# Row maxima subtracted through four array strips, and a new order around it, in a two-layer decoder kernel

## The reference, cut to what matters

```python
def _layernorm(x, axis=-1, eps=1e-05): ...
# 16 heads of 16 channels, 32 sequences of 128 tokens
scores = jnp.einsum('bhqd,bhkd->bhqk', q, k) / math.sqrt(Hd)
probs = jax.nn.softmax(scores, axis=-1)
out = jnp.einsum('bhqk,bhkd->bhqd', probs, v)
...
x = x + _L0_attn_ref(_layernorm(x), ...)                 # self-attention with rotary factors, 16 heads
x = x + _L0_xattn_ref(_layernorm(x), ctx_1024, ...)      # one wide head, tanh of mixed queries and keys
x = x + _L0_ffn_ref(_layernorm(x), ...)                  # routed feed-forward
x = x + _L1_attn_ref(_layernorm(x), ...)                 # self-attention, 16 heads
x = x + _L1_xattn_ref(_layernorm(x), ctx, ctx, mask, ...)# cross-attention, 16 heads, mask over keys
x = x + _L1_ffn_ref(_layernorm(x), ...)                  # ternary feed-forward
```

## Time and profile before

| | us |
|---|---|
| median of 3 runs | 1351.38 (1351.25 to 1352.72) |
| profiled execution | 1354.58 |
| its span (what the rows below count from) | 1352.7 |
| TensorE busy in the span | 1278.7 (95%) |
| VectorE, ScalarE, GpSimd busy | 986.2, 832.0, 468.1 |

### The profile page before, as it was taken

One profiled execution on the slowest core, in us unless ns is written; L12 is line 12 of the kernel. 1 busy time (PEld: TensorE's weight loads), 2 busy tenths in 40 slices (PEclk: granted clock), 3 DMA queues, 4 the chain that ended last, 5 costly groups with the idle time before them and its releaser, 6 DMA issues. The chain is left out here.

```text
span 1352.7 us, 40285 instructions
## 1 busy us (share of the span) xinstructions
PE 1278.7 (95%) x14932; PEld 1153.3 (85%) x14932; DVE 986.2 (73%) x2421; ACT 832.0 (62%) x1659; POOL 468.1 (35%) x576
## 2 busy tenths in 40 slices
PE   6999999899989999998999999999999998699997
PEld 5888888699979999998898888888777877589987
DVE  7888888456655555564888888887877788568886
ACT  4877777455655454553777777666666676356563
POOL 2232232122222122111000000056655567378884
PEclk9999999999988999999999999999999999899999
DMA  6000000031110000001010000000000000000000
GB/s 239 2 3 0 0 1 2 10 116 39 32 32 1 1 0 0 1 1 56 2 65 0 0 0 3 10 18 17 18 16 16 16 9 3 16 9 31 23 30 35
DMA packets 16884, 29.55 MB, mean 22 GB/s; under 512 B 3744, under 2 KB 7840, under 8 KB 16384
## 3 DMA queue, kind: packets, MB, share of 16 engines
q1 hardware_dynamic: 16768, 27.98, 6.3%
HBM read 23.78 MB, written 4.19 MB: 21 GB/s over the span
## 5 line engine op out<-in xcount | busy, mean ns | idle before, releaser
L853 ACT ACTIVATE a_probs<-a_S 128x512 f32<-128x512 f32 x384 | 205.7, 602 | 86.3 <-PE a_S L1314 46.2
L177 POOL TENSOR_TENSOR all_var_eps<-all_moments,all_ln_eps 128x2 f32<-128x2 f32 x96 | 24.3, 253 | 568.3 <-DVE all_moments L172 556.5
L1055 DVE TENSOR_REDUCE a_row_max<-a_S 128x4 bf16<-128x512 f32 x256 | 164.1, 682 | 16.7 <-PE a_S L1252 16.6
L806 POOL TENSOR_TENSOR a_shifts<-a_add_mask,a_cross_max 128x512 bf16<-128x512 bf16 x128 | 141.7, 1133 | 56.8 <-DVE a_cross_max L1055 56.8
L1326 PE MATMUL a_AV<-a_probs,a_v_pad 128*32 128x128 f32 x3072 | 103.8, 276 | 10.1 <-DVE all_odd_split L1068 6.2
L858 ACT ACTIVATE a_av_raw<-a_AV 128x512 f32<-128x512 f32 x96 | 57.5, 599 | 73.0 <-PE a_AV L1326 73.0
L1261 PE MATMUL a_S<-a_qm_hi,all_odd_split 32*128 32x256 f32 x1536 | 94.2, 301 | 6.0 <-DVE a_row_max L1055 2.2
L1326 PEld LDWEIGHTS a_AV<-a_probs,a_v_pad 128*32 128x32 f32 x3072 | 78.1, 109 | 24.8 <-issue 9.8
L105 PE MATMUL c_OUT<-all_odd_split,c_h_hi 128*128 128x256 f32 x512 | 94.6, 283 | 0.9 <-DVE all_x_res L1995 0.9
L1261 PEld LDWEIGHTS a_S<-a_qm_hi,all_odd_split 32*128 32x128 f32 x1536 | 68.9, 183 | 27.1 <-issue 11.6
L1055 DVE TENSOR_REDUCE a_cross_max<-a_S 128x4 f32<-128x512 f32 x128 | 82.6, 682 | 12.1 <-PE a_S L1284 12.1
(11 more groups left out here) (303 smaller groups left out, 4001.5 us busy)
## 6 DMA issues: line engine op xcount, KB each, us to landing
all_cx<-in_ctx_turned SPq DMA_DIRECT2D x16, 256.0 KB, 2.7
all_cx<-in_ctx SPq DMA_DIRECT2D x16, 256.0 KB, 2.7
out_x<-all_x_res SPq DMA_DIRECT2D x16, 256.0 KB, 2.0
all_x_res<-in_x SPq DMA_DIRECT2D x7, 512.0 KB, 7.4
b_routed_wi<-in_L_ffn_wi_W SPq DMA_DIRECT2D x1, 1024.0 KB, 5.2
b_routed_wo<-in_L_ffn_wo_W SPq DMA_DIRECT2D x1, 1024.0 KB, 8.0
all_even_weights<-in_L_ffn_W_fc SPq DMA_DIRECT2D x1, 1024.0 KB, 4.9
all_even_weights<-in_L_ffn_W_proj SPq DMA_DIRECT2D x1, 1024.0 KB, 6.9
```

Source lines behind the costliest of these rows:

```text
L806: pool.tensor_tensor(shifts[:, j], add_mask[:], cross_max[:, j, :].rearrange("p (h o) -> p h o", o=1).to_broadcast([P, QH, P]), ALU.subtra ...
L853: act.activation(probs[:, b * NQ + j, :], S2[j][:], ACT.Exp, scale=DH ** -0.5).then_inc(exp_ok, 1)
L1055: dve.tensor_reduce((cross_max if at(G)[0].cross else row_max)[:, j, :], S1[j][:].rearrange("p (h k) -> p h k", h=QH), AXX, ALU.max).then_ ...
```

## The change

1. **Self-attention layers, both of them.** The maxima of a sequence are kept in a bf16 tile of 128x(4x32), of which 4 columns in each 32 are filled and the rest is zero (set once by GpSimd). A new `turn_maxima` transposes it by one product with the identity into the fourth S1 bank, as soon as the fourth maximum is there. A new `take_rows` on ScalarE copies these 128x128 values to `max_rows`. `shift_scores` then runs 16 products of 32 rows and 128 columns: strip j holds the rows of bank j, the weights are a column of minus one-hot rows broadcast over 128 columns, and the order is by head first and strip second, so that four neighbouring products lie in four strips. The transposes of the coming group move ahead of the shift in these layers too.
2. **Cross-attention.** On VectorE `normalise_x(G + 3)` moves ahead of `normalise`, and `moments_of(G + 4)` right behind it, ahead of the context's low part.
3. **Starts of the stages.** The first sequence's maxima move ahead (`maxima(0, 0, ...)` in group -1); the first moments are taken before the constants are prepared; the fold runs by halves of the weights, each with its own loads and semaphore; the masks of the cross layer are prepared a group later; the first low parts of stage a1 stand in another order.
4. **Filling products.** `fill` issues products of a tile of ones whose result nobody reads: 22 and 11 in the start of a0, 5 and 3 in the start of a1, 4 at the end of both attention stages.
5. The value bias of the cross layer moves behind the shift of the group where it falls.

The diff, cut to its core:

```diff
+def fill(pe, consts, bank, n):
+    for _ in range(n):
+        pe.matmul(bank[:, 0:P], consts["ones"][:], consts["ones"][:], start=True, stop=True, skip_group_check=True)
...
     def fold(self, dve, turn_sign):
-        dve.wait_ge(self.w_ahead, 16 * len(self.ahead))
...
         for k in range(KC):
+            dve.wait_ge(self.w_ahead[k], 16 * len(self.ahead[k]))
...
-    row_max = sb("row_max", [P, 4, QH], BF16)
+    row_max = sb("row_max", [P, 4, 32], BF16)
+    max_rows = sb("max_rows", [P, P], BF16)
...
+            def take_rows(G, b):
+                act.wait_ge(rows_full, G * PAIR + b + 1)
+                at_least(act, s2_full, step(G, b, 0))
+                act.activation(max_rows[:], S1[NQ - 1][:, 0:P], ACT.Copy).then_inc(rows_ok, 1)
...
+                if inside(G) and not at(G)[0].cross:
+                    take_rows(G, 0)
                 for j in range(NQ):
                     if inside(G):
                         exp_step(G, 0, j)
...
+                early = inside(G + 2) and at(G + 2)[0].cross
+                if early and inside(G + 3):
+                    normalise_x(G + 3)
                 if inside(G):
                     normalise(G * PAIR)
+                if early and inside(G + 4):
+                    moments_of(G + 4)
...
+            def turn_maxima(G, b):
+                pe.wait_ge(max_ok, step(G, b, NQ))
+                pe.matmul(S1[NQ - 1][:, 0:P], row_max[:].rearrange("p j h -> p (j h)"), ident_b[:], start=True, stop=True,
+                          skip_group_check=True).then_inc(rows_full, 1)
...
             def shift_scores(G, b):
-                made, n = at(G)[0].cross, at(G)[1]
+                if not at(G)[0].cross:
+                    pe.wait_ge(rows_ok, G * PAIR + b + 1)
+                    for h in range(QH):
+                        for j in range(NQ):
+                            strip = slice(32 * j, 32 * j + 32)
+                            last = pe.matmul(S2[j][:, h * P:(h + 1) * P], minus_rows_b[strip, h:h + 1].to_broadcast([32, P]),
+                                             max_rows[strip, :], start=False, stop=h == QH - 1, skip_group_check=True)
+                            if h == QH - 1:
+                                last.then_inc(s2_full, 1)
+                    return
...
                 if inside(G):
                     scores(G, 0, parity)
+                    if not at(G)[0].cross:
+                        turn_maxima(G, 0)
...
-                if late and normed_here(G + 2):
+                if normed_here(G + 2):
                     transposes(G + 2)
                 if inside(G):
                     shift_scores(G, 0)
-                if not late and normed_here(G + 2):
-                    transposes(G + 2)
```

More of the change, by code:

```diff
@@ L788, in _ @@
         def _(pool):
+            pool.memset(row_max[:], 0.0).then_inc(rows_zero, 1)
             for i in range(2):
@@ L1162, in first_half @@
                 piece(G, 0)
-                if inside(G + 1):
+                if x_dram is None and at_first(G, -1):
+                    low_k(0, odd)
+                    first.norm.dve_low(dve, 1, FA, first.xT_hi[parity], first.xT_lo[parity])
+                    moments_of(2)
+                    for v in range(HV):
+                        low_q(0, odd, v)
+                elif inside(G + 1):
                     if rope:
```

108 lines of the change are left out of this document (64 added, 44 removed).

## The result

| | before, us | changed, us |
|---|---|---|
| median | 1351.53 (6 runs) | 1358.13 (6 runs, 1355.99 to 1359.46) |
| ratio | | 1.0044, 95% interval 1.0032 to 1.0055 |
| profiled execution | 1354.58 | 1355.99 |
| TensorE busy | 1278.7 | 1265.0 |

The change makes the kernel 0.44% **slower**; the forecast was 1346.9, faster, with a range to 1358. The two profiles differ by 1.4 us only, the medians by 6.6: before's profiled execution took longer than all six of its timed runs, and the changed kernel's was its fastest. So the profiles are read here for what single halves do, and the sum is taken from medians.

The account below looks back on a forecast made before the run. TensorE's list was taken to set the self-attention halves, with the exponentials close beside it. Strips +12, norm order -13.5, starts -3 summed to -4.5 us: 1350.1 profiled, 1346.9 median, own range 1341 to 1353, wider range 1335 to 1358.

Parts of the forecast that it names:

- the cross layer's norm order: Cross layer: VectorE's norm and moments move to where it waits for ScalarE; -13.5 us (-6 to -16).
- the starts: Starts of a0 and a1: filling products raise the clock earlier, maxima move ahead; -3 us together (-6 to -1).
- What bounds the kernel: Self-attention halves: the length of TensorE's list sets them, with the exponentials beside it having little room (0.20 us, first half).
- The shift in strips: Self-attention layers: first halves 0.5 us longer, second 0.1 shorter, +0.4 us a group; +12 us in all (+6 to +21).
- The condition for calling the forecast wrong: Wrong if first-half S1 starts before 4.6 us behind S2, or if the cross group stays over 17.6 us.
- get their maxima in time: Self-attention second halves: no change or 0.1 us less, as those overrunning by a VectorE wait get maxima in time.
- 0.9 a group, times 15: Cross layer: 0.55 us plus 0.35 us gained a group, times 15, giving the norm order's -13.5 us.
- GpSimd keeps the cross layer: Rival, 10%: shifts slow beside VectorE, the fourth is late again; only 0.4 goes, -6 us, total 1354.
- S2 first at about 25 in a0: Sign expected in the changed profile: first second scores of a0 at about 25 us; maxima waited for at 26.64 before.
- the value bias costs 0: Value bias behind the shift: the same products, so 0 us, counted within the starts' term.
- Array-bound: Rival, 6%: S1 does not follow the exponentials, TensorE's shorter list pays -12 in place of +12 us; 1323.
- Late exponentials: Rival, 22%, slower: strip rounds take 0.12 us, leaving them is dearer; +21 in place of +12 us; 1356.

Follow-up runs that it names:

- the masks late: Changed kernel with transposes behind the shift in the self layers and the fourth maximum right behind the third in four places: 1343.90 us, ratio 0.9935.
- the masks back: Changed kernel with transposes behind the shift, the fourth maximum ahead, and the cross layer's masks prepared in group -2 again: 1341.58 us, ratio 0.9922.

## Why the prediction was wrong

The forecast lies 11.2 us under the result (1346.9 against 1358.1). Of that, 6.3 come from the cross layer's norm order, 3 to 4 from the starts, nothing from the strips' sum, and 1 to 2 are in no part that was measured alone.

**What bounds the kernel: right.** Starts, not busy time, told it, and the waits for `a_probs` grew as foreseen.

**The shift in strips: the sum right, its parts not.** Forecast +12, measured +11.7 for the strips alone. Of it the regular groups make up less than half: +0.17 to 0.2 a group and not +0.4. The first exponential came at 2.47 and not 2.60, because the strips are cheaper than taken: they start 1.96 behind S2 (forecast 2.00), and their rounds start 0.06 apart, the last one 2.14 behind S2 and not 2.27. The way back to full height costs less too (0.15 from the last strip's start to the next product, 0.2 in the forecast), but that is not on the exponentials' way. From there the third exponential ended 2.05 later (forecast 2.13). The condition for calling the forecast wrong, S1 before 4.6 behind S2, was met by 0.02. What the forecast lacked is the other half. First, **the transposed maxima need the fourth maximum before the first product**. The sentence that the second halves "get their maxima in time" was checked for regular halves and for ScalarE's copy, never for the halves in which something stands between the third and fourth maximum on VectorE: first groups and split weights. Second, the stretch at the lower clock in the second interval (1.6 us in the profile of the strips alone), and third the value bias behind the shift (1.2 us there). Moving the fourth maximum ahead in four places gave back 3.2 us of the changed kernel. That the total agrees is luck, not a success of that term.

**The cross layer's norm order: the step that failed most.** Forecast -13.5 (-6 to -16), measured -7.2 alone and much the same beside the rest. The mechanism held, and in second halves its size too: -0.55 forecast, 9.14 to 8.61 measured. The step that failed is "0.9 a group, times 15". First halves gained 0.19 and not 0.35 (0.24 in the kernel with the norm order alone): over the first eleven groups TensorE's wait for GpSimd's shifts was 3.4 us in 9 places before, 0.31 a group, and 1.0 us in 4 places is left. So a group is worth 0.72, not 0.9, some 2 us in all. The larger part is the 15: the gain shows in 11 groups only, another 3.6 us. The moved calls stand under `inside(G + 3)` and `inside(G + 4)`, so the last three or four groups have none, and the last two that have them gain 0.1 each; in the second half of the last of them S1 to S2 takes 4.07 us in both kernels. The last nine halves together even grew, 81.4 to 82.5, by the stretch at the lower clock in the very last one; a kernel with the same cross layer and the transposes behind has 9.11 there, as before. The rival "GpSimd keeps the cross layer" had -6 for this term, close to what came, but by another way: GpSimd's wait shrank. The lower bound of the range was the better number, and the diff said so.

**The starts: no gain.** Forecast -3 (-6 to -1), measured +0.3 to +1.0 without strips, not told from nothing. "S2 first at about 25 in a0" did not come: the filling products shortened the first projections, and the wait for the norm that follows took it back, with the clock. The second stage's first S2 does come earlier: counted from the last S2 of the first self layer it takes 386.3 to 391.6 us with the new start and 390.1 to 394.6 with the old one (without the strips 388.6, with the norm order alone 391.5). Then interval 0 takes 8.46 instead of 6.82 and the value bias's half 12.24 instead of 11.30. That the value bias costs 0 and that the maxima "move ahead" for nothing were the mistakes: each had something queued behind it. In the first stage the cost of the moved maxima shows only together with the strips.

**Value bias and fills.** The fills are worth nothing measurable in either place. For the value bias two pairs of profiles show +0.9 in its half (11.30 to 12.24 with the old shift, 11.52 to 12.46 with strips), the medians don't tell.

**The rivals.** Array-bound was refuted by the changed kernel's own profile: S1 starts 0.06 behind the third exponential, after a wait of 0.63. It is not reached with the transposes behind either, where S1 still waits 0.23 and two regular halves take 14.44 us against 14.64 before, half of what that rival had. "Late exponentials", which gave 1356, was the outcome in sign and time, but not by its mechanism: rounds of strips cost not 0.12 us but about half of it. The Trainium skill, "TensorE: Matmul & The Clock Gate", gives a least distance of about 25 ns between two starts (section "Wait — 56ns, not 53.3ns?"), which the forecast held against the strips. By that figure sixteen starts would need an estimated 0.375 us; the trace does not agree, all sixteen stand within 0.19. Another section of that page of the Trainium skill, "Part 3: Packing small matmuls", has about 4 ns between products in different row strips. With this the trace agrees: the four starts of a round are 3 to 5 ns apart. The forecast had overlooked it.

**Still open.** Why the first group of the second stage still takes 8.0 us with the masks in their old place. Its clock stays up; two waits for VectorE, 0.32 and 0.42 us, show in it, and the rest of the 1.2 was not followed. Open too is what makes the lower clock come in one kernel and not in another with the same list.

## What to carry to other kernels

A step that turns four small dependences into one (here: transpose all maxima, then shift) starts at the last of the four: look on the producing engine for every place in the program where something stands between the third and the fourth, not only at the loop. A cheaper operation on the busiest engine is worth its saving only if its first result does not come later: put what is long and urgent to nobody, the transposes here, behind it. Count in how many groups a moved call exists before multiplying. And where TensorE already waits, a longer wait can cost more than its length: look at the clock of what stands behind it.

## What the runs showed that was not expected

- **Strips of 32 rows and 128 columns in bf16** run in rounds of 0.056 us, four products for the time of one full-height product of the same width (0.056); from the last strip's start to the next full-height product it takes 0.15 us, 0.33 from the first strip on.
- **Steps of 1.5 us by the clock.** The second interval of a stage is either near 7.0 or near 8.5 us in kernels with the same list there (8.52 with the masks late and 6.99 with the masks back, in the first self layer), and the long ones have TensorE's clock at 0.50, as in 662.60 to 666.00 above. The last interval of the cross layer has the same two values, 9.1 and 10.4 to 10.9. One profile of a kernel can therefore mislead by several us. Whether such steps also make the scatter between runs of one kernel (1356.0 to 1359.5 for the changed one) is not shown, since each was profiled once.
- **A shorter wait ahead of S1 was given back whole**: with S1 0.5 us earlier, the half grew by 0.1, as the same move delayed an input of the projection behind it.
